# A fused RWKV block and mixture of experts: x loaded feature-major, its layer norm folded into scaled weights and a scale per token

## The reference

```python
x = x + attn(layernorm(x))          # an RWKV block, which has layer norms of its own
x = x + moe(layernorm(x))

# attn(x0), with x0 = layernorm(x)
xn1 = layernorm(x0) * g1 + b1
r = sigmoid(xn1 @ Wr.T); w = -exp(xn1 @ Ww.T); k = xn1 @ Wk.T; v = xn1 @ Wv.T
num = decay * num + exp(w + k) * v  # over the 512 tokens of a sequence
den = decay * den + exp(w + k)
a = x0 + (r * num / (den + 1e-8)) @ Wo.T
xn2 = layernorm(a) * g2 + b2
a + sigmoid(xn2 @ Wrec.T) * (relu(xn2 @ Wkey.T)**2 @ Wval.T)

# moe(h): a shared gated FFN of width 512, and 16 experts of width 128, of which each
# token uses the one with the largest logit, scaled by the sigmoid of that logit
```

## Time and profile before

| | |
|---|---|
| median of 3 runs | 493.52 us |
| the profiled execution | 494.78 us, of which the span of instructions 492.7 us |
| TensorE matmul (PE) busy | 477.8 us, 97% |
| TensorE weight load (PEld) busy | 389.2 us, 79% |
| VectorE (DVE) busy | 370.5 us, 75% |
| GpSimd (POOL) busy | 353.4 us, 72% |
| ScalarE (ACT) busy | 323.4 us, 66% |
| mean granted TensorE clock | 0.994 of full |
| DMA | 39.33 MB, 80 GB/s over the span |

### The profile page before, as it was taken

How to read it: one execution, slowest core, us unless ns; L and a number is a source line. 1 busy time by engine, 2 the same in 40 slices (tenths; PEclk the granted TensorE clock), 3 DMA queues, 4 the chain that set the end, 5 groups by cost and what they waited for, 6 DMA issues and landing times.

```text
span 492.7 us, 10517 instructions
## 1 busy us (share of the span) xinstructions
PE 477.8 (97%) x3093; PEld 389.2 (79%) x3093; DVE 370.5 (75%) x1056; ACT 323.4 (66%) x623; POOL 353.4 (72%) x573
## 2 busy tenths in 40 slices
PE   8897999999999999999999999999999999999994
PEld 6654868777778687786877867888899999999994
DVE  6989799899999999996899989847445555545534
ACT  3665778978878879787687986554355555555430
POOL 6665588898888988986688877677226676667750
PEclk9999899999999999999999999999999999999998
DMA  7007001101011021010101001111389654542037
GB/s 236 2 4 274 23 1 64 34 35 64 23 44 58 10 65 43 23 66 21 45 23 43 34 11 45 45 44 37 115 195 259 190 157 135 150 136 69 24 77 266
DMA packets 33031, 39.33 MB, mean 80 GB/s; under 512 B 4913, under 2 KB 29113, under 8 KB 32720
## 3 DMA queue, kind: packets, MB, share of 16 engines
q1 hardware_dynamic: 26640, 24.98, 17.4%
q0 software_dynamic: 5760, 13.16, 7.7%
q10 hardware_dynamic: 576, 0.52, 0.3%
HBM read 21.69 MB, written 17.93 MB: 80 GB/s over the span
## 4 chain that ended last, share of the span: by engine, by line
PE 78%; DVE 5%; issue 5%; POOL 5%; DMA 4%; ACT 1%; SPq 1%; POOLq 0%; DVEq 0%; ACTq 0%
PE bank L424 17%; PE bank L417 10%; PE bank L441 6%; PE bank L411 4%; PE bank L804 3%; PE bank L805 3%; PE bank L797 3%; PE bank L432 3%; PE bank L521 3%; PE bank L507 3%; PE bank L533 3%; PE bank L512 3%; PE bank L517 3%; PE bank L699 2%; PE bank L668 2%
## 5 line engine op out<-in xcount | busy, mean ns | idle before, releaser
L424 PE MATMUL bank<-hT,wm 128*128 128x256 f32 x512 | 124.7, 384 | 0.6 <-ACT kr L890 0.6
L424 PEld LDWEIGHTS bank<-hT,wm 128*128 128x128 f32 x512 | 92.6, 191 | 19.2 <-issue 9.0
L1498 POOL DMA_INDIRECT sorted_rows<-rows,posi x64 | 72.5, 1132 | 19.6 <-issue 16.9
L1580 POOL DMA_INDIRECT out<-shared x55 | 53.8, 979 | 36.7 <-DVE shared L1412 19.8
L417 PEld LDWEIGHTS bank<-wm,k 128*128 128x128 f32 x512 | 61.9, 192 | 8.1 <-issue 7.1
L417 PE MATMUL bank<-wm,k 128*128 128x128 f32 x512 | 62.3, 276 | 0.0
L1054 ACT ACTIVATE er<-bank 128x256 f32<-128x256 f32 x40 | 15.3, 383 | 44.9 <-PE bank L805 44.3
L1420 DVE TENSOR_TENSOR e<-er,bank 128x256 f32<-128x256 f32 x40 | 16.9, 422 | 23.0 <-ACT er L1054 20.5
L441 PE MATMUL bank<-wm,actA 128*128 128x128 f32 x240 | 32.9, 281 | 0.0
L921 ACT ACTIVATE h<-rows,smE 128x128 f32<-128x128 f32 x64 | 26.3, 482 | 8.5 <-POOL smE L1474 8.5
L1580 POOL DMA_INDIRECT out<-rows x24 | 23.5, 977 | 11.0 <-issue 6.8
(11 more groups left out here) (256 smaller groups left out, 1294.3 us busy)
## 6 DMA issues: line engine op xcount, KB each, us to landing
shared<-sorted_rows SPq DMA_DIRECT2D x56, 128.5 KB, 2.3
shared<-x SPq DMA_DIRECT2D x16, 256.0 KB, 3.7
rows<-sorted_rows SPq DMA_DIRECT2D x24, 128.5 KB, 2.8
wexp<-w_exp SPq DMA_DIRECT2D x2, 1536.0 KB, 8.8
sorted_rows<-filler SPq DMA_DIRECT2D x17, 128.5 KB
shared<-out SPq DMA_DIRECT2D x6, 256.0 KB, 5.7
out<-shared SPq DMA_DIRECT2D x12, 128.0 KB, 2.7
sorted_rows<-rows,posi POOLq DMA_INDIRECT x64, 2.6
```

The source lines that it names most:

```text
L424: ins = mm(dst[:, j * HALF:(j + 1) * HALF], W(name, 2 * pair_ + j), src[:, half * HALF:(half + 1) * HALF], start=True, stop=True)
L1498: g_.indirect_dma_start(sorted_ap, bass.IndirectOffsetOnAxis(posi[t % 3][:, g:g + 1].bitcast(U32), 0), rows[t % 3][:, g, :], None).then_in ...
L1580: g_.indirect_dma_start(out, bass.IndirectOffsetOnAxis(xr[k % RING][:, j, D:D + 1].bitcast(U32), 0), xr[k % RING][:, j, D + 1:ROW], None, ...
```

## The change

Tiles 0 and 1 are handled as before (`BY_TOKEN = 2`). For the other 14 tiles:

- x is also given to the kernel as a second array x_feat, feature-major, and SP loads each tile of it (256 KB) into one buffer, `feat`, that takes the place of xn1tok[0]. The transposes T1, the scaling of x to xn1tok and the copy with g1 and b1 go.
- SP stores the tile's 512 scales (smA index 4, 128 partitions by 4) to a row in DRAM, waits until that has landed, and loads the row into all 128 partitions, `rs_all`, in place of xn1tok[1]. VectorE multiplies feat by it (`scaled_x`) right behind q.
- The mean is taken out by the weights: during tiles 0 and 1 the weights Ww, Wk, Wr, Wv are scaled by g1 on ScalarE, multiplied by a centring matrix (identity minus 1/128) on TensorE and written back over wm. The products of the four weights with b1 become four shifts per feature, that enter as bias of the exps and as scalar of the operations of z and ev.
- norm_a moves from VectorE to ScalarE, behind the last square of the round and ahead of silu0. For that GpSimd makes two more small quantities in smC, the negative mean and its product with the scale.
- One semaphore of tile 8's second half goes (hD0), others are renamed or shared.

```diff
+            def load_feat(t):
+                wait(sp, "T1", 0)
+                if t > BY_TOKEN:
+                    wait(sp, "xn1T", t - 1)
+                sp.dma_start(feat[:, :], x_feat[:, t * T:(t + 1) * T]).then_inc(s["rs_in"], 16)
+
+            def spread_scales(t):
+                wait(sp, "pA", t)
+                sp.dma_start(rs_rows[t:t + 1, :].rearrange("o (p g) -> (o p) g", g=G), smA[t % 3][:, 4, :]).then_inc(s["vec_rs"], 16)
+                sp.wait_ge(s["vec_rs"], 16 * (t - BY_TOKEN + 2))
+                wait(sp, "T1", BY_TOKEN - 1)
+                sp.dma_start(rs_all[:, :], rs_rows[t:t + 1, :].to_broadcast([P, T])).then_inc(s["rs_in"], 16)
+
+            for t in range(BY_TOKEN, XR):
+                load_feat(t)
+                spread_scales(t)
             for t in range(XR, NT):
                 load_x(t)
+                if t > XR:
+                    load_feat(t - 1)
+                    spread_scales(t - 1)
...
+            load_feat(NT - 1)
+            spread_scales(NT - 1)
...
-                for t in at(1):
+                for t in [t for t in at(1) if t < BY_TOKEN]:
                     if t == 1:
                         warm(WARM_BEFORE[0])
                     wait(pe, "xn1tok", t)
...
                     mm(V_B[:, :], W("Wv"), xn1T[t % 2][:, :], start=True, stop=True).then_inc(s["Vp"], 1)
+                    if t == 0:
+                        pe.wait_ge(s["w_fold"], 2)
+                        for i, name in enumerate(("Ww", "Wk", "Wr", "Wv")):
+                            ins = mm(SMALL[:, i:i + 1], W(name), V("b1"), start=(i == 0), stop=True, skip_group_check=True)
+                        ins.then_inc(s["w_fold"], 1)
+                    if t == BY_TOKEN - 1:
+                        pe.wait_ge(s["w_fold"], 4)
+                        mm(SMALL[:, :], centre[:, :], raw_w[:, :], start=True, stop=True).then_inc(s["w_fold"], 1)
...
+            def norm_a(t):
+                wait(act_e, "pC", t)
+                wait(act_e, "T2", t - 2)
+                for g in range(G):
+                    ins = af(grp(an[t % 2], g), grp(a[t % 2], g), ACT.Identity, bias=smC[t % 3][:, 3, g:g + 1],
+                             scale=smC[t % 3][:, 1, g:g + 1])
+                ins.then_inc(s["an"], 1)
...
+                    if t == 0:
+                        af(raw_w[:, :], wm[:, 0:4 * D], ACT.Copy, scale=V("g1")).then_inc(s["w_fold"], 1)
...
                     square3(t)
+                for t in at(3):
+                    if t == 0:
+                        act_e.wait_ge(s["w_fold"], 5)
+                        af(wm[:, 0:4 * D], SMALL[:, :], ACT.Copy).then_inc(s["w_fold"], 1)
+                    norm_a(t)
                 for t in at(5, A_TILES):
                     silu0(t)
...
+            def scaled_x(t):
+                dve.wait_ge(s["rs_in"], 32 * (t - BY_TOKEN + 1))
+                wait(dve, "Vp", t - 2)
+                v.tensor_tensor(by_group(xn1T[t % 2]), by_group(feat),
+                                rs_all[:, :].rearrange("p (i g) -> p g i", g=G), ALU.mult).then_inc(s["xn1T"], 1)
...
-                for t in at(3):
-                    norm_a(t)
...
                     v.scalar_tensor_tensor(q[t % 2][:, :], den[t % 2][:, :], WKV_EPS, er[t % 2][:, :], ALU.add, ALU.mult).then_inc(s["q"], 1)
+                for t in at(1):
+                    if t >= BY_TOKEN:
+                        scaled_x(t)
                 for t in at(5, A_TILES):
                     act0(t)
...
                 for t in at(4):
                     wait(gp, "agC", t)
+                    wait(gp, "an", t - 3)
+                    g_.tensor_scalar(smC[t % 3][:, 2, :], mvC[t % 3][:, :, 0], -1.0, 0.0, ALU.mult, ALU.add)
                     rstd(smC[t % 3], mvC[t % 3], "pC", t)
+                    wait(gp, "pC", t, 2)
+                    g_.tensor_tensor(smC[t % 3][:, 3, :], smC[t % 3][:, 2, :], smC[t % 3][:, 1, :], ALU.mult).then_inc(s["pC"], 1)
```

More of the change, by code:

```diff
@@ L79 @@
 WHO = {}
+BY_TOKEN = 2
+for _n in ("xn1tok", "T1"):
+    WHO[_n] = range(BY_TOKEN)
 for _n in ("G0", "U0", "sg0", "ac0", "G1", "U1", "sg1", "ac1", "D1", "base"):
     WHO[_n] = A_TILES
-for _n in ("hG0", "hU0", "hsg0", "hac0", "hD0", "hG1", "hU1", "hsg1", "hac1", "hD1", "hbase"):
+for _n in ("hG0", "hU0", "hsg0", "hac0", "hG1", "hU1", "hsg1", "hac1", "hD1", "hbase"):
     WHO[_n] = B_TILES
@@ L362, in _ @@
             load_x(0)
-            sp.dma_start(vec[:, :], vecs).then_inc(s["v_in"], 16)
+            sp.dma_start(vec[:, :], vecs).then_inc(s["vec_rs"], 16)
             load_x(1)
@@ L937, in one_round @@
                     tanh_of_max(t)
-                for t in at(2):
+                for t in [t for t in at(2) if t < BY_TOKEN]:
                     wait(act_e, "pA", t)
@@ L985, in one_round @@
                     wait(act_e, "q", t - 2)
-                    af(er[t % 2][:, :], R_B[:, :], ACT.Exp, scale=-1.0).then_inc(s["er1"], 1)
+                    if t < BY_TOKEN:
+                        af(er[t % 2][:, :], R_B[:, :], ACT.Exp, scale=-1.0).then_inc(s["er1"], 1)
+                    else:
+                        af(er[t % 2][:, :], R_B[:, :], ACT.Exp, bias=shift[:, 4:5], scale=-1.0).then_inc(s["er1"], 1)
                 for t in at(4):
@@ L1386, in late_step @@
                         wait(dve, f"cD{step}", NT)
-                        wait(dve, f"hD{step}", NT)
+                        wait(dve, "hD1", NT)
                     v.tensor_tensor(late_act(u)[step][:, :], late_sg(u)[step][:, :], late_bank(u, step)[1][:, :], ALU.mult).then_inc(s["lac"], 1)
@@ L1521, in one_round @@
                         wait(gp, "pA", t, 1)
-                        g_.tensor_tensor(sm[:, 3:5, :], sm[:, 1:3, :], half8[:, :, :], ALU.pow).then_inc(s["pA"], 1)
-                        wait(gp, "pA", t, 2)
-                        g_.tensor_tensor(sm[:, 5, :], sm[:, 0, :], sm[:, 4, :], ALU.mult).then_inc(s["pA"], 1)
+                        g_.tensor_tensor(sm[:, 3:5, :], sm[:, 1:3, :], half8[:, :, :], ALU.pow).then_inc(s["pA"], 1 if t < BY_TOKEN else 2)
+                        if t < BY_TOKEN:
+                            wait(gp, "pA", t, 2)
+                            g_.tensor_tensor(sm[:, 5, :], sm[:, 0, :], sm[:, 4, :], ALU.mult).then_inc(s["pA"], 1)
                 for t in at(5):
```

52 lines of the change are left out of this document (35 added, 17 removed).

## The result

The changed kernel takes 511.44 us (median of 4 runs, 510.40 to 512.66); beside it the kernel before takes 493.22 (median of 4). The ratio is 1.0366, 95% interval 1.0345 to 1.0387. So the change costs 18 us, where the prediction said -1. The profiled execution has a span of 510.0 us against 492.7.

The account below looks back on a forecast made before the run. TensorE was taken as the bound of equal 19.55 us rounds, with a new DMA loop then exceeding it. Terms -5.2 - 1.8 + 6.0 = -1.0 us gave 493.8 profiled, 492.5 us by the median; range 486 to 500.

Parts of the forecast that it names:

- The loop of xa: From one end of xa through DMAs, VectorE and GpSimd to the next: 19.98 us against TensorE's 19.12, costing 6.0 us.
- the term "6.8": Three loads and a store on SP's queue, from xa's end to the scales' landing: 6.8 us, bounds 5.4 to 7.8.
- the second rival: At the spreading load ahead of act0: scales land later than forecast, at 7.8 us giving 499.5 us; chance 0.27.
- seven periods: Rounds from after 60 us to before 216 us, each paying 0.86 us for the loop, 6.0 us in all.
- the long round: The 25.62 us round of the tile with a second half of shared work; expected to give back 4 us of slack.
- the -5.2 of the transposes: On TensorE, twelve groups of transposes of x at 0.43 us each drop out, saving 5.2 us.
- 2.0 us of cover: In middle rounds, normalised a is ready at 96.9 and its transposes stand at 98.94, so the norm's move costs 0.
- the rival that the norm is late for its transposes: ScalarE's norm of a misses TensorE's transposes by 0.5 us in each of 12 rounds: 498.5 us; chance 0.05.
- the first rival: In the rounds TensorE stays the bound, scales arriving in under 5.9 us: -7.0 us, 486.5 us; chance 0.23.
- The stall for h: Near 49.22 us TensorE had waited 2.15 us for h; the wait was to vanish and the clock hold.
- -1.8: At the start, TensorE reaches the gates at 51.3 instead of 53.12, 1.8 us earlier; bounds -3.9 to +2.1.

Follow-up runs that it names:

- the turned kernel: Changed kernel with SP's feature-major load, scale store and spreading load for tile t-1 ahead of the load of x for t: 498.08 us, ratio 1.0107.
- the run with many rows: Changed kernel, but the last DMA loads 128 different rows of x_feat instead of one row of scales 128 times: 504.78 us, ratio 1.024.

## Why the prediction was wrong

*The mechanism was right, its size was not.* The time measured, 511.4 us, lies 11 above the end of the predicted range. The loop of xa, load of x, store, spreading load, product, act0, scan, GpSimd, xa is the bound, as said, and turning SP's list takes 13 us off. The step that failed first is the term "6.8" from xa to the landing of the scales. It was 8.1. The issues and the store took 3.56 of it (4.15 predicted) and the spreading load 4.57, for which I took a load of x as the nearest row. I named "one DRAM row is read 128 times" as a reason for the second rival and still left it at 2.65; the run with many rows gave 3.0. Nothing in the trace of before showed such a read, and it should have moved the value taken, not only the range. What the runs show in its place: 4.57 us from issue to use for the one row beside GpSimd's scatters, 3.00 for 128 rows in the same place, and 3.6 from issue to landing for the one row without scatters. The estimate by the Trainium skill's rule in DMA: Bandwidth & Descriptors, "Anatomy of one DMA", was 2.6 for the same load, and the measurement decides against it here as against my number.

*The product* was costed at 0.6 with bounds 0.6 to 1.2, and is 1.02, by the step of four. Taken alone that is 0.4 a round.

*The number of rounds.* I let the loop pay in seven periods and the others run at 19.12, because the long round would give back slack. It gave none: TensorE is held at its keys by act0 and act1 of the same round, so I read that a lag is stored nowhere. Measured: eight periods ahead of the long round at 21.46 and the one behind it at 21.7. Against 19.12 these nine are 8 x 2.34 + 2.6 = 21.3 us, where the prediction had 6.0. With the -5.2 of the transposes and +0.65 for the start that is 16.8 us, beside the 17.3 of span measured.

*What was costed at 0.* This was ScalarE's norm (0, with 2.0 us of cover for the transposes of a); for GpSimd's small operations I had +0.3, which no term of the sum took up. The cover held: the rival that the norm is late for its transposes did not come in the middle rounds. But I asked only who waits for the norm, and not what stands behind it on ScalarE, which is silu (so act0) and the copy for xn2T. The scan blocks GpSimd, as I had used in the loop, and I did not apply it to the two operations that I added there. By the runs with SP's list turned and without the scales' DMA this makes the difference between the predicted 486.5 of the first rival and the measured 498: that rival's premise (TensorE stays the bound) was wrong even without the DMAs. On the same footing the gain for TensorE was 0.13 us a round (19.55 to 19.42) and not 0.43. Not all of these 12 us are explained by a test; by the trace they go so: three collisions of the power and the scan in the turned kernel are 3, the missing 0.3 in nine rounds another 3, the start 2.6, and about 3 lie in the round before the last two tiles (21.4 us where the kernel before has 17.9), whose cause stays open.

*The start.* The stall for h went, as said. But the two waits for a were followed by a lower clock: behind 1.24 us for a and 0.87 for xn2T it was 0.50 from 44 to 46 us and 0.68 to 48, so -1.8 became +0.65 at the gates. I had carried the delay and assumed the clock.

The second rival, "the scales come later still", is what happened: it was placed right, at the spreading load, with 7.8 us as its upper term and 499.5 us. Its own sum fell short by the terms above: 8.1 instead of 7.8, the longer product, and nine rounds instead of seven.

## What to carry over

A loop that closes over several engines and queues has to be summed with each member's real duration, and one member of a kind that the trace does not show deserves its upper bound; and such a loop pays in every round, unless a buffer lets a lag be carried. Before a step is moved to an engine with idle time, list who stands behind it there, and what the removed work had covered: here 0.43 us of transposes taken out of a round gave 0.13 at best. The version to prefer is the kernel before; of the variants that compute the whole reference the turned list was the best, 1.1 to 1.2% above it.

## What the runs showed of the hardware

- A load of one DRAM row into 128 partitions was slower than one of 128 rows with as many bytes: 4.57 against 3.00 us from issue to use while GpSimd's scatters ran, with the DMA engines busy at 74 GB/s; 3.6 against 3.0 from issue to landing (medians) without them.
- A VectorE product of 128x512 float32 whose second operand is read with a step of four values takes 1.09 us, with step one 0.69.
- A store of 512 pieces of 4 B held SP's next issue for 10 us, one of 128 pieces of 16 B for 1.4 on an otherwise empty queue and 2.55 behind two loads (one round each). The small pieces made the kernel 11 us longer.
- A GpSimd power of 128x4 took 2.04 us where VectorE's scan started 0.07 us after it, and 1.02 where it started 0.13 after it.
- Chips differ, and in the turned kernel, which ran on two, in one part only. Up to the last xa it took 330.6 us on the one and 328.4 on the other; from there to the end, in the expert part, 165.1 and 185.4. The same stretch on both, first the faster chip:

```profile
330.00:495.00 165.00, 159.77 (x1169) 150.26 (x1167) 84.69 (x204) 77.80 (x181) 97.55 (x110) 1.00 0.48 138
```

```profile
330.00:495.00 165.00, 151.82 (x1062) 138.68 (x1061) 73.13 (x180) 69.52 (x169) 94.23 (x105) 0.98 0.41 113
```

On the second chip ScalarE's exps of the expert part wait up to 5.8 us at a time (29.8 us in eight waits, besides 24.1 in 14 for TensorE); on the first none of their 35 waits is over 1.6 us (44.5 us together). What makes them wait was not found.
